# A set's four groups of states side by side in one row, products with C by halves of the time axis, in an SSM and FP4 FFN kernel

## The chip, the cores and the metric

One core of a Trainium2 chip runs the whole program. The metric is the device time in microseconds (us) of one execution. The kernel before takes 343.71 us (median of three runs, 343.64 to 343.86).

## The reference, cut to what matters

```python
# x: (4, 1024, 128); 16 states per channel
u = silu(conv3(x));  Bc, Cc = split(u @ W_bc + b_bc);  dt = softplus((u @ W_dt + b_dt) @ W_dtp + b_dtp)
h[t] = exp(A * dt[t]) * h[t-1] + Bc[t] * x[t] * dt[t]      # for each of 128 channels and 16 states
y[t] = sum_n Cc[t, n] * h[t, n] + x[t] * Dcoeff
x1 = layernorm(x + y)
out = layernorm(x1 + fp4_linear(silu(fp4_linear(x1, w_gate)) * fp4_linear(x1, w_up), w_down))
# fp4_linear: blocks of 16 of both operands are rounded to the FP4 grid, then multiplied
```

## The kernel before, in words

The 4096 rows are eight units of 512 time steps (UNIT), two to a batch. The 128 channels times 16 states are 16 groups (GROUPS) of 128 rows: four sets (SETS) of four groups (QUADS); one group holds 32 channels times four states. Each engine has its own instruction list, written out by hand as `step(b, a, s, f, g, h, p)` with 16 slots `k`; the dictionary `AT` (line 84) says in which slot an operation stands on its engine. In step i the scans of unit s = i run; a and b are the units after it, being prepared; f, g and h are the units one, two and three before it, whose norm, quantised FFN and output run in the gaps. An engine works through its list in order and waits at semaphores, so a slot is an order, not a time.

The parts that matter here:

- **ScalarE (ACT)**, line 541: `decay` writes exp(A dt) of one group to one of three PSUM banks.
- **VectorE (DVE)**, line 1122: `times_b` makes B x dt of one set (`db`) from the bank `ps_b` and the replicated dt x. `scan` (line 1133) runs the recurrence of one group over 512 steps, its second operand from PSUM, and writes `states`. Set m of `times_b` stands in slots 15 (of the step before), 3, 7 and 11. Line 1089 is the limiting of FP4 codes (`h quant 5` of unit g in slot 8).
- **GpSimd (POOL)**, line 869: `times_c` multiplies two groups of states with C (`c_rep`), 1024 elements a partition, in each odd slot, after two more scans. Beside it POOL does the elementwise steps of both quantisations: lines 904, 893, 898, 912 for x of unit f, lines 918, 893, 898, 928 for the hidden layer of unit g (its sum in slot 13, its codes, line 898, in slot 15 behind the last product, `hq` in slot 0 of the next step).
- **TensorE (PE)**, line 1401: `sum_states` adds a set's products over its states into `ps_y` with four matmuls. The sums of the last two sets stand in slot 0 of the next step; there they are followed by `spread_b` (line 1452) of set 1, which fills `ps_b` for the next `times_b`.

`states0` holds 16 groups, `states1` six in a ring; `product` holds two sets. In the last step the last set is multiplied with C on DVE (`times_last_c`, line 1210), and PE goes on with `sum_of_last`.

Of the kernel before, what the change touches and what calls it, by code (L numbers as in the profile page):

```python
# [51 lines left out]
def bank_of(unit, k):  # L52
# [9 lines left out]
PRODUCTS = 2 * SET_PAIRS  # L62
ODD_STATES = 6
X1 = 3
# [18 lines left out]
AT = {  # L83
    "pe x": 11, "pe conv": (13,), "pe z": 15, "pe B": (13, 1, 5, 10), "pe C": (5, 6, 8, 10),
    "pe sum": (8, 11, GROUPS, GROUPS), "pe r": 2, "pe xq": 12, "pe gate": (13, 13, 14, 14),
    "pe up": (15, 15, GROUPS, GROUPS), "pe hq": 4, "pe down": (7, 8), "act x": 12, "act window": 15,
    "act C": (4, 7, 9, 10), "act r": 0, "act r variance": 3, "act x1": 3, "act xq": 12, "act hq": 3,
    "act variance": 10, "act y": 11, "act x square": 7, "act h square": 7, "dve db": (15, 3, 7, 11), "dve dtx": 1,
    "dve tiles": (GROUPS, GROUPS, GROUPS + 1, GROUPS + 1),
    "dve x quant": {0: (4, False), 1: (5, True), 2: (5, False), 5: (9, False)},  # L90
    "dve h quant": {0: (1, False), 1: (4, False), 2: (5, True), 5: (8, False)}, "pool x norm": 3, "pool xq": 8,
    "pool h norm": 4, "pool h sum": 13, "pool h codes": 15, "pool hq": GROUPS,
}


FIRST = {**AT,
    "pe x": 0, "pe conv": (1, 2), "pe z": 3, "pe C": (7, 9, 10, 11), "act x": 0, "act window": 4,
    "act C": (7, 8, 9, 11), "dve dtx": 6,
}
# [78 lines left out]


def over(t, n):  # L180

    return t.rearrange("p (a t) -> p a t", a=1).broadcast_to([t.shape[0], n, t.shape[1]])


def build(nc, x, conv_w, w_bc, b_bc, w_dt, b_dt, w_dtp, b_dtp, a_log, dcoeff, w_gate, w_up, w_down, out):
# [6 lines left out]
    with ctx:  # L192
# [50 lines left out]
        db = [sb(f"db{j}", [128, QUADS, UNIT]) for j in range(DB)]  # L243
        states = [sb("states0", [128, GROUPS, UNIT]), sb("states1", [128, ODD_STATES, UNIT])]
        product = sb("product", [128, PRODUCTS, 2, UNIT])

        conv_0 = product[:, 0, 0, :]
        wdt_t, wdtp = (states[1][0:RANK, 3, i * D:(i + 1) * D] for i in range(2))

# [34 lines left out]
        def flat(t):  # L284
            return t.rearrange("p q d -> p (q d)")
# [4 lines left out]

        spare = flat(states[0][:])
        in_use = 3 * TILES * INNER + TILES * 3 * 128
# [33 lines left out]

        last_states = [states[1][:], dt_rep[0][:].rearrange("p c i t -> p (c i) t"), c_rep[0][:]]

        def groups(s, k, n):

            if s.first < UNITS - 1:
                t = states[s.first % 2]
                k %= t.shape[1]
                return t[:, k:k + n, :]
            for t in last_states:
                if k < t.shape[1]:
                    return t[:, k:k + n, :]
                k -= t.shape[1]

# [516 lines left out]
        def _(pool):  # L856
# [143 lines left out]
        def _(dve):  # L1000
# [132 lines left out]
            def scan(s, k, p):  # L1133
                ring = states[p].shape[1]

                if s.first == UNITS - 1 and k >= ring:

                    if k == ring + 2 * QUADS:
                        dve.wait_ge(product_done, s.at(PAIRS))
                elif p == 1 and k >= ring:  # L1140
                    dve.wait_ge(product_done, s.at(PAIRS, (k - ring) // 2 + 1))
                elif s.beyond(2):
                    dve.wait_ge(product_done, s.at(PAIRS, (k - ring - GROUPS) // 2 + 1))
# [5 lines left out]
                nc.vector.tensor_tensor_scan(  # L1149
                    out=groups(s, k, 1)[:, 0, :], data0=ps_decay[BANK_OF[s.at(GROUPS, k)]][:],  # L1150
                    data1=db[k // QUADS % DB][:, k % QUADS, :],
                    initial=states[0][:, k, UNIT - 1:UNIT] if p else 0.0,
                    op0=ALU.mult, op1=ALU.add).then_inc(scan_done, 1)
# [56 lines left out]
            def times_last_c(s, k):  # L1210


                j = k // 2
                dve.wait_ge(scan_done, s.at(GROUPS, k + 1))
                dve.wait_ge(prep_evac, s.at(PREP_EVAC, PREP_EVAC))
                dve.wait_ge(sum_done, s.at(SETS, (j - PRODUCTS) // SET_PAIRS + 1))
                nc.vector.scalar_tensor_tensor(
                    out=product[:, j % PRODUCTS, k % 2, :], in0=ps_prep[:], scalar=bbc_rep[:, 1, SETS - 1:SETS],
                    in1=groups(s, k, 1)[:, 0, :],
                    op0=ALU.add, op1=ALU.mult).then_inc(last_product, 1)  # L1220
# [136 lines left out]
        def _(pe):  # L1357
# [43 lines left out]
            def sum_states(s, m, p):  # L1401
# [186 lines left out]
            def tail(f, g, h, p):  # L1588
                def sum_of_last():

                    m = SETS - 1
                    for c in range(QUADS):
                        pe.wait_ge(last_product, c + 1)
                        last = nc.tensor.matmul(ps_y[c * E:(c + 1) * E, :], gather[:],
                                                product[:, (m * SET_PAIRS + c // 2) % PRODUCTS, c % 2, :],
                                                start=False, stop=True)
# [101 lines left out]
```

## Time and profile before

| | |
|---|---|
| runs, median | 343.71 us |
| the profiled execution | 346.96 us, of which its span on the core 345.2 us |
| DVE busy | 302.5 us (88%) |
| POOL busy | 268.8 us (78%) |
| PE busy, weight loads | 263.9 us (76%), 131.0 us (38%) |
| ACT busy | 248.0 us (72%) |
| products with C on POOL (line 878) | 139.6 + 7.3 us in 62 instructions |
| scans on DVE (line 1149) | 151.4 us of DVE, more with the last unit's |
| chain that ended last | POOL 45%, DVE 16%, issue 12%, PE 12%, ACT 9% |

Busy time is that of instructions on an engine. The middle 60% of the span consists of steps that repeat each 35 us; the rest is a head of about 20 us in which nothing is there yet to scan, and a tail of some 45 us after the last scan. A step begins for DVE with the first scan of its unit. The chain of waits is followed back from the last instruction; where two engines are both busy without a gap, it stays on the one that it is on, so its shares don't tell by themselves which of the two bounds.

### The profile page before, as it was taken

To read this page: it belongs to the slowest core of one execution; us is meant where nothing else is said; L and a number is where in the kernel's file an instruction comes from. 1 tells how busy PE (TensorE), PEld (TensorE's weight loads), DVE (VectorE), ACT (ScalarE), POOL (GpSimd) and SP (SyncE) were. 2 spreads that over 40 slices of the span, in tenths; PEclk is the share of its full clock that TensorE was granted. 3 is DMA by queue.
4 is the path that set the end of the run, shared out by engine and by line. 5 is a ranking of instruction groups with operands and counts; after the bars stand their busy time and mean duration, and the time that the engine had idled before them with its cause. 6 is when DMAs were issued, how large, how long until landed. Compare 5 with 4: busy or idle time off the path is not lost.

```text
span 345.2 us, 3946 instructions
## 1 busy us (share of the span) xinstructions
PE 263.9 (76%) x1130; PEld 131.0 (38%) x1130; DVE 302.5 (88%) x327; ACT 248.0 (72%) x538; POOL 268.8 (78%) x146
## 2 busy tenths in 40 slices
PE   2679976678758879798999888787849667967683
PEld 1223322224313434353534344334324433355582
DVE  3868998999999999999999999999996999756920
ACT  3466889658855987989879988888874866354434
POOL 0084665688279998999899999999999799846632
PEclk9956999989996999989899999999987995969678
DMA  3680663800380028021802190109010001000002
GB/s 50 151 205 0 139 139 76 197 0 0 71 184 22 3 54 191 0 61 34 195 17 62 38 206 1 30 19 207 19 31 2 0 0 31 2 0 12 19 2 62
DMA packets 19262, 21.86 MB, mean 63 GB/s; under 512 B 6112, under 2 KB 15144, under 8 KB 19240
## 3 DMA queue, kind: packets, MB, share of 16 engines
q1 hardware_dynamic: 18520, 21.05, 26.9%
q10 hardware_dynamic: 720, 0.56, 0.9%
q8 instruction: 9, 0.15, 0.2%
q14 instruction: 13, 0.11, 0.1%
HBM read 2.72 MB, written 2.10 MB: 14 GB/s over the span
## 4 chain that ended last, share of the span: by engine, by line
POOL 45%; DVE 16%; issue 12%; PE 12%; ACT 9%; DMA 1%; ACTq 1%; SPq 1%; DVEq 0%; POOLq 0%
POOL product L878 22%; DVE states L1149 6%; DVE db L1129 6%; POOL qh_norm L918 4%; POOL qh_magic L898 4%; POOL qh_norm L893 4%; POOL hq L928 4%; ACT ps_decay L548 2%; ACT L538 2%; POOL qx_norm L904 2%; POOL qx_magic L898 2%; POOL qx_norm L893 2%; POOL xq L912 2%; PE ps_prep L1437 1%; DMA dt_rep<-dtx 1%
## 5 line engine op out<-in xcount | busy, mean ns | idle before, releaser
L878 POOL TENSOR_TENSOR product<-states,c_rep 128x1024 f32<-128x1024 f32 x59 | 139.6, 2383 | 24.8 <-DVE states L1149 21.9
L548 ACT ACTIVATE ps_decay<-dt_rep,aneg 128x512 f32<-128x512 f32 x128 | 87.1, 691 | 25.6 <-DVE states L1149 18.4
L1149 DVE TENSOR_TENSOR_SCAN states<-ps_decay,db 128x512 f32<-128x512 f32 x64 | 74.9, 1201 | 0.3
L1129 DVE SCALAR_TENSOR_TENSOR db<-ps_b,bbc_rep,dt_rep 128x2048 f32<-128x2048 f32 x31 | 72.1, 2326 | 1.4 <-PE ps_b L1456 1.4
L1149 DVE TENSOR_TENSOR_SCAN states<-ps_decay,states,db 128x512 f32<-128x512 f32 x54 | 66.6, 1260 | 1.0 <-ACT ps_decay L548 1.0
L1450 PE MATMUL ps_prep<-u_feat,wbc_rep 128*128 128x512 f32 x56 | 33.4, 680 | 11.8 <-ACT c_rep L625 11.2
L1456 PE MATMUL ps_b<-u_feat,wbc_rep 128*128 128x512 f32 x64 | 38.1, 680 | 5.1 <-DVE db L1129 5.1
L1414 PE MATMUL ps_y<-product,gather 128*32 128x512 f32 x248 | 33.5, 629 | 4.0 <-POOL product L878 4.0
L538 ACT ACT_TABLE_LOAD x25 | 32.1, 1283 | 0.5
L1495 PE MATMUL ps_f<-gate_t,xq_t 128*128 128x352 f32 x48 | 19.7, 537 | 6.8 <-ACT hidden L632 5.7
L625 ACT ACTIVATE c_rep<-ps_prep,bbc_rep 128x512 f32<-128x512 f32 x28 | 19.2, 684 | 7.3 <-PE ps_prep L1450 7.3
L1437 PE MATMUL ps_prep<-x_feat,tap_diag 128*128 128x512 f32 x42 | 21.8, 653 | 2.3 <-issue 1.3
L1541 PE MATMUL ps_f<-ident,hq 128*128 128x128 f32 (+1 forms) x60 | 10.1, 292 | 12.3 <-POOL hq L928 9.4
L1187 DVE TENSOR_TENSOR hidden<-hidden,ps_f 128x352 f32<-128x352 f32 x26 | 13.1, 515 | 7.3 <-PE ps_f L1501 5.2
L928 POOL TENSOR_TENSOR hq<-qh_magic,qh_scale 128x1408 f32<-128x1408 bf16 x7 | 18.1, 2583 | 0.6
L1450 PEld LDWEIGHTS ps_prep<-u_feat,wbc_rep 128*128 128x128 f32 x56 | 9.3, 202 | 24.2 <-ACT c_rep L625 21.9
L1456 PEld LDWEIGHTS ps_b<-u_feat,wbc_rep 128*128 128x128 f32 x64 | 11.3, 206 | 18.5 <-issue 10.5
L1501 PE MATMUL ps_f<-up_t,xq_t 128*128 128x352 f32 x48 | 18.3, 512 | 0.0
L918 POOL TENSOR_TENSOR qh_norm<-hidden,qh_inv 128x1408 f32<-128x1408 f32 x7 | 18.1, 2592 | 0.0
L898 POOL TENSOR_TENSOR qh_magic<-qh_norm,qh_magic 128x1408 bf16<-128x1408 f32 x6 | 17.2, 2870 | 0.1
L893 POOL TENSOR_TENSOR qh_norm<-qh_norm,qh_magic 128x1408 f32<-128x1408 f32 x6 | 17.2, 2859 | 0.0
L1527 PE MATMUL ps_f<-down_t,hq_t 128*128 128x128 f32 (+1 forms) x120 | 16.7, 275 | 0.0
(237 smaller groups left out, 506.1 us busy)
## 6 DMA issues: line engine op xcount, KB each, us to landing
dt_rep<-dtx SPq DMA_DIRECT2D x124, 128.0 KB, 2.4
x_tok<-in_L_attn_x SPq DMA_DIRECT2D x8, 256.0 KB, 2.9
out<-y_out SPq DMA_DIRECT2D x7, 256.0 KB, 2.3
dt_rep<-dtx ACTq DMA_DIRECT2D x4, 128.0 KB, 3.7
out<-y_out SPq DMA_DIRECT2D x2, 128.0 KB, 2.0
hidden<-in_L_ffn_w_down SPq DMA_DIRECT2D x1, 176.0 KB, 3.5
x_feat<-in_L_attn_x SPq DMA_DIRECT2D x8, 0.5 KB, 2.1
hidden<-in_L_ffn_w_gate SPq DMA_DIRECT2D x1, 128.0 KB, 2.8
```

The lines of the kernel that those rows point to most:

```text
L538: act.add_instruction(mybir.InstLoadActFuncSet(act_func_set_id=which, name=nc.get_next_instruction_name(), engine=mybir.EngineType.Activat ...
L548: nc.scalar.activation(ps_decay[BANK_OF[i]][:], dt_rep[p][:, c, 0, :], ACT.Exp, scale=aneg[:, c, m:m + 1]).then_inc(decay_done, 1)
L878: nc.gpsimd.tensor_tensor(product[:, j % PRODUCTS], groups(s, 2 * j, 2), over(c_rep[p][:, j // SET_PAIRS, :], 2), ALU.mult).then_inc(produ ...
L893: order.mark(nc.gpsimd.tensor_tensor(b.norm[:, 0:width], b.norm[:, 0:width], b.magic[:, 0:width], ALU.add))
L898: order.mark(nc.gpsimd.tensor_tensor(b.magic[:, 0:width], b.norm[:, 0:width], b.magic[:, 0:width], ALU.subtract))
L918: nc.gpsimd.tensor_tensor(blocked(qh.norm[:]), blocked(flat(hidden[:])), spread_out(qh.inv[:]), ALU.mult).then_inc(h_norm_done, 1)
L928: nc.gpsimd.tensor_tensor(blocked(flat(hq[:])), blocked(qh.magic[:]), spread_out(qh.scale[:]), ALU.mult).then_inc(hq_done, 1)
L1129: nc.vector.scalar_tensor_tensor(out=db[m % DB][:], in0=over(ps_b[:], QUADS), scalar=bbc_rep[:, 0, m:m + 1], in1=dt_rep[p][:, :, 1, :], op ...
L1149: nc.vector.tensor_tensor_scan(out=groups(s, k, 1)[:, 0, :], data0=ps_decay[BANK_OF[s.at(GROUPS, k)]][:], data1=db[k // QUADS % DB][:, k % ...
L1414: last = nc.tensor.matmul(ps_y[c * E:(c + 1) * E, :], gather[:], product[:, (m * SET_PAIRS + c // 2) % PRODUCTS, c % 2, :], start=False, s ...
L1450: nc.tensor.matmul(ps_prep[:], wbc_rep[:, 1, m], u_feat[o][:], start=True, stop=True).then_inc(prep_mm, 1)
L1456: nc.tensor.matmul(ps_b[:], wbc_rep[:, 0, m], u_feat[o][:], start=True, stop=True).then_inc(b_mm, 1)
```

## The change

The states of a set are laid out time step by time step, the four groups' values of one time step next to each other (16 bytes). A scan writes its 512 values with a stride of four elements; the product of a set is contiguous again, and is made in two instructions of 256 time steps times four groups, in which the value of C is repeated four times (`beside`) where it was a row repeated twice (`over`). Both need all four scans of the set, and both stand in slots 3, 7, 11 and 15, one before and one after the other operations of that slot. PE's sums read `product` with a stride of four elements, `times_last_c` reads and writes so. `states1` holds eight groups, and its ring is given free set by set. Slots: PE's `spread_b` of set 1 from 1 to 2, r from 2 to 4, x's transposes from 12 to 13, the fourth gate matmul from 14 to 15; ACT's r from 0 to 1; DVE's `h quant 5` from 8 to 11; POOL's h sum from 13 to 12; and three slots of the first unit.

```diff
-ODD_STATES = 6
+SIDE = QUADS
+ODD_STATES = 8
...
-    "pe x": 11, "pe conv": (13,), "pe z": 15, "pe B": (13, 1, 5, 10), "pe C": (5, 6, 8, 10),
-    "pe sum": (8, 11, GROUPS, GROUPS), "pe r": 2, "pe xq": 12, "pe gate": (13, 13, 14, 14),
+    "pe x": 11, "pe conv": (13,), "pe z": 15, "pe B": (13, 2, 5, 10), "pe C": (5, 6, 8, 10),
+    "pe sum": (8, 11, GROUPS, GROUPS), "pe r": 4, "pe xq": 13, "pe gate": (13, 13, 14, 15),
-    "act C": (4, 7, 9, 10), "act r": 0, "act r variance": 3, "act x1": 3, "act xq": 12, "act hq": 3,
+    "act C": (4, 7, 9, 10), "act r": 1, "act r variance": 3, "act x1": 3, "act xq": 12, "act hq": 3,
-    "dve h quant": {0: (1, False), 1: (4, False), 2: (5, True), 5: (8, False)}, "pool x norm": 3, "pool xq": 8,
-    "pool h norm": 4, "pool h sum": 13, "pool h codes": 15, "pool hq": GROUPS,
+    "dve h quant": {0: (1, False), 1: (4, False), 2: (5, True), 5: (11, False)}, "pool x norm": 3, "pool xq": 8,
+    "pool h norm": 4, "pool h sum": 12, "pool h codes": 15, "pool hq": GROUPS,
...
+def beside(t, n):
+
+    return t.rearrange("p (t a) -> p t a", a=1).broadcast_to([t.shape[0], t.shape[1], n])
...
-        states = [sb("states0", [128, GROUPS, UNIT]), sb("states1", [128, ODD_STATES, UNIT])]
-        product = sb("product", [128, PRODUCTS, 2, UNIT])
+        states = [sb("states0", [128, GROUPS // SIDE, UNIT, SIDE]), sb("states1", [128, ODD_STATES // SIDE, UNIT, SIDE])]
+        product = sb("product", [128, PRODUCTS * 2 * UNIT])
+        products = product[:].rearrange("p (m t c) -> p m t c", t=UNIT, c=SIDE)
...
             def times_c(s, j, p):
-                pool.wait_ge(scan_done, s.at(GROUPS, 2 * j + 2))
+                m, half = j // SET_PAIRS, slice(j % SET_PAIRS * UNIT // 2, (j % SET_PAIRS + 1) * UNIT // 2)
+                pool.wait_ge(scan_done, s.at(GROUPS, QUADS * m + QUADS))
...
-                nc.gpsimd.tensor_tensor(product[:, j % PRODUCTS], groups(s, 2 * j, 2),
-                                        over(c_rep[p][:, j // SET_PAIRS, :], 2), ALU.mult).then_inc(product_done, 1)
+                nc.gpsimd.tensor_tensor(products[:, m % 2, half], beside_each_other(s, QUADS * m)[:, half],
+                                        beside(c_rep[p][:, m, half], SIDE), ALU.mult).then_inc(product_done, 1)
...
                 for k in range(GROUPS):
-                    if s is not None and k % 2 and (a is not None or k < GROUPS - QUADS):
-                        times_c(s, k // 2, p)
+                    products = s is not None and k % QUADS == QUADS - 1 and (a is not None or k < GROUPS - QUADS)
+                    if products:
+                        times_c(s, k // 2 - 1, p)
                     if g is not None:
                         quant(g, k)
...
                     if h is not None:
                         quant(h, k + GROUPS)
+                    if products:
+                        times_c(s, k // 2, p)
...
                 elif p == 1 and k >= ring:
-                    dve.wait_ge(product_done, s.at(PAIRS, (k - ring) // 2 + 1))
+                    dve.wait_ge(product_done, s.at(PAIRS, ((k - ring) // QUADS + 1) * SET_PAIRS))
...
                 nc.vector.tensor_tensor_scan(
-                    out=groups(s, k, 1)[:, 0, :], data0=ps_decay[BANK_OF[s.at(GROUPS, k)]][:],
+                    out=state(s, k), data0=ps_decay[BANK_OF[s.at(GROUPS, k)]][:],
                     data1=db[k // QUADS % DB][:, k % QUADS, :],
...
                     last = nc.tensor.matmul(ps_y[c * E:(c + 1) * E, :], gather[:],
-                                            product[:, (m * SET_PAIRS + c // 2) % PRODUCTS, c % 2, :],
+                                            product_of(m, c),
                                             start=False, stop=(m == SETS - 1))
```

## Rows read from the trace of the kernel before

**Rows 1.** Windows, step 5: length, busy of PE, PEld, DVE, ACT, POOL

```profile
204.68:239.51 34.83, 29.19 (x141) 14.30 (x141) 34.28 (x34) 30.11 (x67) 34.00 (x17) 1.00 0.30 67
```

**Rows 2.** DVE's timeline: start us, us, engine, line, operation, idle before and releaser

```profile
222.82 1.27 DVE L1149 TENSOR_TENSOR_SCAN states<-ps_decay,states,db 128x512 f32<-128x512 f32 x1
224.01 1.19 DVE L1149 TENSOR_TENSOR_SCAN states<-ps_decay,db 128x512 f32<-128x512 f32 x1
225.65 1.11 DVE L1187 TENSOR_TENSOR hidden<-hidden,ps_f 128x352 f32<-128x352 f32 x2 [0.45 <-PE ps_f L1501]
...
232.10 2.32 DVE L1129 SCALAR_TENSOR_TENSOR db<-ps_b,bbc_rep,dt_rep 128x2048 f32<-128x2048 f32 x1
```

**Rows 3.** POOL's timeline of the same stretch

```profile
223.61 2.85 POOL L893 TENSOR_TENSOR qh_norm<-qh_norm,qh_magic 128x1408 f32<-128x1408 f32 x1
226.43 2.37 POOL L878 TENSOR_TENSOR product<-states,c_rep 128x1024 f32<-128x1024 f32 x1
228.75 2.87 POOL L898 TENSOR_TENSOR qh_magic<-qh_norm,qh_magic 128x1408 bf16<-128x1408 f32 x1
...
239.51 1.06 POOL L904 TENSOR_TENSOR qx_norm<-x,qx_inv 128x512 f32<-128x512 f32 x1 [0.59 <-DVE qx_inv L1077]
```

**Rows 4.** PE there: weights of the last sum, then the matmul for `times_b`

```profile
228.84 0.27 PEld L1414 LDWEIGHTS ps_y<-product,gather 128*32 128x32 f32 x8 [0.58 <-POOL product L878]
229.96 1.12 PE L1456 MATMUL ps_b<-u_feat,wbc_rep 128*128 128x512 f32 x2
```

**Rows 5.** Groups of POOL's instructions: xcount | busy us, mean ns | idle before

```profile
L878 POOL TENSOR_TENSOR product<-states,c_rep 128x1024 f32<-128x1024 f32 x59 | 139.6, 2383 | 24.8 <-DVE states L1149 21.9 <-PE ps_y L1414 2.9
L918 POOL TENSOR_TENSOR qh_norm<-hidden,qh_inv 128x1408 f32<-128x1408 f32 x7 | 18.1, 2592 | 0.0
L893 POOL TENSOR_TENSOR qh_norm<-qh_norm,qh_magic 128x1408 f32<-128x1408 f32 x6 | 17.2, 2859 | 0.0
...
L904 POOL TENSOR_TENSOR qx_norm<-x,qx_inv 128x512 f32<-128x512 f32 x7 | 7.4, 1060 | 7.5 <-DVE qx_inv L1077 7.5
```

**Rows 6.** DVE's timeline at another boundary of steps, and at the last one

```profile
152.85 1.27 DVE L1149 TENSOR_TENSOR_SCAN states<-ps_decay,states,db 128x512 f32<-128x512 f32 x1
...
162.39 2.33 DVE L1129 SCALAR_TENSOR_TENSOR db<-ps_b,bbc_rep,dt_rep 128x2048 f32<-128x2048 f32 x1
...
257.29 1.21 DVE L1149 TENSOR_TENSOR_SCAN states<-ps_decay,db 128x512 f32<-128x512 f32 x1
...
268.22 2.32 DVE L1129 SCALAR_TENSOR_TENSOR db<-ps_b,bbc_rep,dt_rep 128x2048 f32<-128x2048 f32 x1
```

**Rows 7.** Timeline of step 2 about slots 8 to 11

```profile
104.73 0.89 DVE L1089 TENSOR_SCALAR qh_magic<-qh_magic 128x1408 bf16<-128x1408 bf16 x1
...
105.54 1.21 DVE L1149 TENSOR_TENSOR_SCAN states<-ps_decay,db 128x512 f32<-128x512 f32 x1
...
106.83 1.91 PE L1456 MATMUL ps_b<-u_feat,wbc_rep 128*128 128x512 f32 x2
...
108.79 2.35 DVE L1129 SCALAR_TENSOR_TENSOR db<-ps_b,bbc_rep,dt_rep 128x2048 f32<-128x2048 f32 x1 [0.59 <-PE ps_b L1456]
```

**Rows 8.** The same two operations in step 6

```profile
246.12 1.02 PE L1456 MATMUL ps_b<-u_feat,wbc_rep 128*128 128x512 f32 x2
...
248.33 2.32 DVE L1129 SCALAR_TENSOR_TENSOR db<-ps_b,bbc_rep,dt_rep 128x2048 f32<-128x2048 f32 x1
```

**Rows 9.** Timeline of the tail: POOL's hq and PE around it

```profile
298.27 2.58 POOL L928 TENSOR_TENSOR hq<-qh_magic,qh_scale 128x1408 f32<-128x1408 bf16 x1
...
299.84 0.76 PE L1520 MATMUL ps_f<-up_t,xq_t 128*128 128x352 f32 x2
...
300.90 0.66 PE L1541 MATMUL ps_prep<-ident,hq 128*128 128x128 f32 x4 [0.30 <-POOL hq L928]
```

**Rows 10.** Groups of DVE's instructions: a scan, a product of the last set

```profile
L1149 DVE TENSOR_TENSOR_SCAN states<-ps_decay,db 128x512 f32<-128x512 f32 x64 | 74.9, 1201 | 0.3
...
L1217 DVE SCALAR_TENSOR_TENSOR product<-ps_prep,bbc_rep,dt_rep 128x512 f32<-128x512 f32 x2 | 1.5, 750 | 0.1
```

More of the change, by code:

```diff
@@ L90 @@
     "dve x quant": {0: (4, False), 1: (5, True), 2: (5, False), 5: (9, False)},
-    "dve h quant": {0: (1, False), 1: (4, False), 2: (5, True), 5: (8, False)}, "pool x norm": 3, "pool xq": 8,
-    "pool h norm": 4, "pool h sum": 13, "pool h codes": 15, "pool hq": GROUPS,
+    "dve h quant": {0: (1, False), 1: (4, False), 2: (5, True), 5: (11, False)}, "pool x norm": 3, "pool xq": 8,
+    "pool h norm": 4, "pool h sum": 12, "pool h codes": 15, "pool hq": GROUPS,
 }
 FIRST = {**AT,
-    "pe x": 0, "pe conv": (1, 2), "pe z": 3, "pe C": (7, 9, 10, 11), "act x": 0, "act window": 4,
-    "act C": (7, 8, 9, 11), "dve dtx": 6,
+    "pe x": 0, "pe conv": (1, 3), "pe z": 3, "pe C": (6, 9, 10, 11), "act x": 0, "act window": 4,
+    "act C": (7, 8, 10, 11), "dve dtx": 6,
 }
@@ L243, in build @@
         db = [sb(f"db{j}", [128, QUADS, UNIT]) for j in range(DB)]
-        states = [sb("states0", [128, GROUPS, UNIT]), sb("states1", [128, ODD_STATES, UNIT])]
-        product = sb("product", [128, PRODUCTS, 2, UNIT])
-        conv_0 = product[:, 0, 0, :]
-        wdt_t, wdtp = (states[1][0:RANK, 3, i * D:(i + 1) * D] for i in range(2))
+        states = [sb("states0", [128, GROUPS // SIDE, UNIT, SIDE]), sb("states1", [128, ODD_STATES // SIDE, UNIT, SIDE])]
+        product = sb("product", [128, PRODUCTS * 2 * UNIT])
+        products = product[:].rearrange("p (m t c) -> p m t c", t=UNIT, c=SIDE)
+        conv_0 = product[:, 0:UNIT]
+        wdt_t, wdtp = (states[1][0:RANK, 0, :, :].rearrange("p t c -> p (t c)")[:, i * D:(i + 1) * D] for i in range(2))
         r_feat = sb("r_feat", [128, UNIT])
@@ L288, in build @@
         wraw, wquant = flat(hidden[:])[:, 0:WCOLS], flat(hq[:])[:, 0:WCOLS]
-        spare = flat(states[0][:])
+        spare = states[0][:].rearrange("p q t c -> p (q t c)")
         in_use = 3 * TILES * INNER + TILES * 3 * 128
@@ L324, in build, with beside_each_other, state, product_of @@
         last_q = [tail_quant(i, last_gate[i][:, 0:INNER] if i in in_bank else tail_norm[:, i]) for i in range(TILES)]
-        last_states = [states[1][:], dt_rep[0][:].rearrange("p c i t -> p (c i) t"), c_rep[0][:]]
-        def groups(s, k, n):
+        last_states = [states[1][:], dt_rep[0][:].rearrange("p c i t -> p (c i t)")
+                       .rearrange("p (q t c) -> p q t c", t=UNIT, c=SIDE)]
+        def beside_each_other(s, k):
             if s.first < UNITS - 1:
                 t = states[s.first % 2]
-                k %= t.shape[1]
-                return t[:, k:k + n, :]
+                return t[:, k // SIDE % t.shape[1]]
             for t in last_states:
-                if k < t.shape[1]:
-                    return t[:, k:k + n, :]
-                k -= t.shape[1]
+                if k < t.shape[1] * SIDE:
+                    return t[:, k // SIDE]
+                k -= t.shape[1] * SIDE
+        def state(s, k):
+            return beside_each_other(s, k)[:, :, k % SIDE]
+        def product_of(m, c):
+            k = m * QUADS + c
+            return products[:, k // SIDE % (PRODUCTS * 2 // SIDE), :, k % SIDE]
         def gate_bank(f, i):
@@ L1133, in scan @@
             def scan(s, k, p):
-                ring = states[p].shape[1]
+                ring = states[p].shape[1] * SIDE
                 if s.first == UNITS - 1 and k >= ring:
-                    if k == ring + 2 * QUADS:
-                        dve.wait_ge(product_done, s.at(PAIRS))
+                    pass
                 elif p == 1 and k >= ring:
-                    dve.wait_ge(product_done, s.at(PAIRS, (k - ring) // 2 + 1))
+                    dve.wait_ge(product_done, s.at(PAIRS, ((k - ring) // QUADS + 1) * SET_PAIRS))
                 elif s.beyond(2):
-                    dve.wait_ge(product_done, s.at(PAIRS, (k - ring - GROUPS) // 2 + 1))
+                    dve.wait_ge(product_done, s.at(PAIRS, ((k - ring - GROUPS) // QUADS + 1) * SET_PAIRS))
                 dve.wait_ge(decay_done, s.at(GROUPS, k + 1))
@@ L1149, in scan @@
                 nc.vector.tensor_tensor_scan(
-                    out=groups(s, k, 1)[:, 0, :], data0=ps_decay[BANK_OF[s.at(GROUPS, k)]][:],
+                    out=state(s, k), data0=ps_decay[BANK_OF[s.at(GROUPS, k)]][:],
                     data1=db[k // QUADS % DB][:, k % QUADS, :],
-                    initial=states[0][:, k, UNIT - 1:UNIT] if p else 0.0,
+                    initial=states[0][:, k // SIDE, UNIT - 1:UNIT, k % SIDE] if p else 0.0,
                     op0=ALU.mult, op1=ALU.add).then_inc(scan_done, 1)
@@ L1217, in times_last_c @@
                 nc.vector.scalar_tensor_tensor(
-                    out=product[:, j % PRODUCTS, k % 2, :], in0=ps_prep[:], scalar=bbc_rep[:, 1, SETS - 1:SETS],
-                    in1=groups(s, k, 1)[:, 0, :],
+                    out=product_of(SETS - 1, k % QUADS), in0=ps_prep[:], scalar=bbc_rep[:, 1, SETS - 1:SETS],
+                    in1=state(s, k),
                     op0=ALU.add, op1=ALU.mult).then_inc(last_product, 1)
@@ L1594, in sum_of_last @@
                         last = nc.tensor.matmul(ps_y[c * E:(c + 1) * E, :], gather[:],
-                                                product[:, (m * SET_PAIRS + c // 2) % PRODUCTS, c % 2, :],
+                                                product_of(m, c),
                                                 start=False, stop=True)
```

## The prediction

> **What bounds the kernel now.** I read the page first (busy shares, chain), then windows of one step, then the timeline of DVE, POOL and PE at the boundary of two steps, last the tail. The page's chain runs 45% through POOL and invites the thought that POOL is the bound. The window says otherwise: in a step of 34.83 us DVE is busy 34.28 us and POOL 34.00 us [rows 1]. Two engines are full, and the timelines tell which waits for which. DVE's only wait is 0.45 us for a matmul of PE [rows 2]. POOL waits 0.59 us, for DVE's reciprocal [rows 3]. DVE never waits for POOL. So DVE sets the step, and POOL keeps up with about 0.6 us to spare. A cheaper product on POOL buys nothing in the middle, and what must be asked is what the later place of the products makes late.
>
> **The product itself.** Today 1024 elements take 2383 ns [rows 5]. The reads stay contiguous for the states, and C is repeated innermost. The nearest row with an innermost repeat is line 904/918: 1060 ns for 512 and 2592 ns for 1408, so 1.71 ns per further element, and 1060 + 512 x 1.71 = 1.94 us for 1024. That repeat is 16 long, here it is 4, so 1.94 is the low end unless a repeat of 4 is cheaper than one of 16, which nothing suggests. The high end is no gain, 2.36 us, today's in the timeline [rows 3]; a start for each short run of four could even pass that, and each 0.1 us more costs what 0.1 us less saves below. Line 893 (one operand half as wide) takes 2859 ns for 1408, between the two. I take 1.94, as the nearest in form. From start to start today's product takes 2.32 us (226.43 to 228.75 [rows 3]), the new one then 1.90.
>
> The Trainium skill, GPSIMD Engine Reference, section 2.1, says that a two-input operation has its operands share one read port and so costs about 2.5 cycles an element, whatever is repeated. An estimate from that page at its 1.2 GHz is 2.1 ns an element, which today's product fits and line 918 does not; by it the product stays as it is.
>
> **The boundary of two steps, where the change costs.** Today the last product needs the last two scans and stands alone ahead of POOL's codes (line 898); its sum follows on PE, and behind that sum in PE's list stands `spread_b` of set 1, which DVE's second `times_b` waits for. In the trace: product until 228.80, PE takes the sum at 228.84, the matmul for `times_b` runs from 229.96 to 231.08, and DVE comes to it at 232.10 [rows 2 to 4]: 1.0 us to spare. After the change both halves need scan 15, and the codes stand between them. The new path, from the end of scan 15 (222.82 + 1.27 = 224.09 [rows 2]): start of POOL 0.08 (an estimate from the gap between engines), product 1.90, codes 2.82 (the 2.85 to 2.87 us operations take 2.82 from start to start [rows 3]), product 1.94, start of PE 0.04, sum 1.12, matmul 1.12 [rows 4], start of DVE 0.05: 9.07 us. DVE's own path to that `times_b` is 232.10 - 224.09 = 8.01 us [rows 2]. So DVE waits 1.06 us. At another boundary its path is 162.39 - 152.85 - 1.27 = 8.27 us [rows 6], wait 0.80. Moving `spread_b` from slot 1 to 2 alters nothing, the sum is ahead of it either way.
>
> How often: the codes exist from step 2 on, and the last boundary has a path of 268.22 - 257.29 - 1.21 = 9.72 us [rows 6], longer than 9.07, because its hidden tiles come late. That leaves the ends of steps 2, 3, 4 and 5: four boundaries, at a mean of the two waits of 0.93: **+3.7 us**. Boundaries 0 and 1 have no codes: 2.82 less, no wait. The work that starts from DVE or from the sum (r, x1, the quantisations) moves with the wait; PE's r one matmul later (1.12) meets a DVE that is 1 us later too.
>
> **Step 2, slots 8 to 11.** `h quant 5` moves from ahead of `times_b` of set 3 to behind scan 11. In step 2 that `times_b` waits 0.59 us for PE already, whose matmul ends at 106.83 + 1.91 = 108.74 [rows 7]. This is set by ACT and PE (slow there), not by DVE. The 0.81 us of the moved operation (104.73 to 105.54 [rows 7]) was cover for that wait; it now stands behind it: **+0.8 us**. In step 6 the matmul ends at 247.14 and DVE comes at 248.33 [rows 8], 1.19 us of slack, which pays for it; there, and in the steps like it, zero, at most 0.3.
>
> **The tail.** In the last step POOL's two products before h's sum are 2 x 0.42 us shorter, so `hq` ends some 0.9 us before today's 300.85. But PE's list has the up matmul ahead of its transposes, until 300.60 [rows 9]; the transposes start 0.3 us earlier and no more: **-0.3 us**. `times_last_c` now reads and writes with a stride. It takes 0.75 us, and if it fell to a scan's pace 1.20 us [rows 10], four would cost 1.8 us, all on the path to the last sum. Zero and 1.8 are the ends; I take zero, as its other operand comes from PSUM and one stream from SBUF is left.
>
> **Scans and sums with a stride.** A scan takes 1.20 us for 512, 2.35 ns an element [rows 10], where `times_b` writes one element every 2.32/2048 = 1.14 ns [rows 2]. A write that costs twice would still hide in the scan's pace. I take zero. The sums read with a stride; no row shows such a matmul. From nothing to a doubling (+1.12 each); zero taken, the doubling is a rival.
>
> The ring of `states1` grows from six to eight groups and is freed set by set: scan 8 waits for set 0, whose second half ends before set 1's scans do; scan 12 for set 1. No wait. The rest of the slots (gate, xq, first unit) pass nothing that the rows show to be late: zero.
>
> **The sum.** 3.7 + 0.8 - 0.3 = +4.2 us. The profiled execution has 345.2 us of span in 346.96; with +4.2 it would be 349.4 in 351.2. The median of the runs is 343.71, 3.25 under that, so **347.9 us**.
>
> **The rivals.**
> 1. *The product is no quicker* (2.36 us). For it: a repeat of four is short. Two products in each of four paths, 8 x 0.42 = +3.4 us: 351.3 us. Between the two, with line 893's rate, about 349.4. POOL would then have no idle time.
> 2. *PE's strided reads cost.* Every value that a sum reads lies 16 bytes behind the one before; if that halves the rate, a sum takes 2.24 instead of 1.12 us, 4 x 1.12 = 4.5 at the boundaries and 1.1 in the tail: 347.9 + 5.6 = 353.5 us. Against it: the four matmuls read the same 16 bytes side by side. The Trainium skill (SBUF — State Buffer, the note on SBUF cachelines) has this rule: lines are 16 bytes, and a read that meets a new line each time pays a penalty; by it the sums, the scans and `times_last_c` would all be slower.
> 3. *Scans slow down*, if a strided write costs three times 1.14 ns: 3.42 x 512 = 1.75 us, +0.55 each on the engine that bounds, for 128 scans +70 us: 414 us. Against it: a factor of two still hides.
> 4. *Not slower: the boundary closes.* Without products, the path is 9.07 - 3.84 = 5.23 us, so it fits into 8.14 (the mean of the two) if two products take 2.9 us, 1.45 us each: the point from which it decides. It would need 1.3 ns an element, under every row. Then 343.7 + 0.8 - 0.3 = 344.2 us; and if step 2's PE also comes sooner and `hq`'s whole 0.9 us counts, 342.8. The page's chain, so much on POOL, speaks for it, the waits [rows 2, 3] against.
>
> **How the numbers follow.** The forecast (346.9 to 349.5) has 0.46, rival 1 0.16, rival 2 0.12, rival 3 0.05, rival 4 0.21: 0.09 at 344.2, 0.12 at 342.8. 0.2% (0.7 us) is about what a measurement of this kernel can tell from no change; so faster 0.12, same 0.09, slower 0.79. The range leaves out rival 3 and the lower half of rival 4, and runs from 343.6 to 353.8.
>
> **What would show it.** In the profile after: product (line 878's successor) near 1.94 us; POOL busy some 30.6 us of each step, 34.0 less 8 x 0.42; DVE's `times_b` of set 1 with about 1 us idle ahead of it, released by PE `ps_b`, four times; between the two last products 2.9 us of codes; scans at 1.20 and 1.27, sums at 1.1. Wrong would be: `times_b` without a wait there (then the path is shorter than I think), or longer scans, or sums with long matmuls, or a step still of 34.8 us.

## The result and the profile after

The changed kernel takes 357.81 us, the kernel before 343.78 us in the same comparison: a ratio of 1.039, 95% interval 1.035 to 1.043. Slower, as forecast, but by 14.0 us and not by 4.2, and above the range (343.6 to 353.8). One of the four executions of after took 1318.5 us, for a reason that nothing here shows; the ratio is taken over the other three. The profiled execution of after took 356.63 us with a span of 354.8.

The page of after, busy times:

```profile
PE 278.4 (78%) x1130; PEld 124.2 (35%) x1130; DVE 304.7 (86%) x327; ACT 247.9 (70%) x538; POOL 248.0 (70%) x146
```

POOL does 20.8 us less than before (268.8), PE 14.5 us more (263.9), DVE 2.2 us more (302.5). DVE, which sets the step, now idles 50.1 us of its span where it idled 42.7: it waits more. The groups of POOL, PE and DVE of after, each with its count, its busy time and mean, and the idle time ahead:

```profile
L895 POOL TENSOR_TENSOR product<-states,c_rep 128x1024 f32<-128x1024 f32 x60 | 121.3, 2039 | 62.9 <-DVE states L1168 62.7
...
L1433 PE MATMUL ps_y<-product,gather 128*32 128x512 f32 x248 | 61.3, 1071 | 7.6 <-POOL product L895 7.5
...
L1149 DVE SCALAR_TENSOR_TENSOR db<-ps_b,bbc_rep,dt_rep 128x2048 f32<-128x2048 f32 x31 | 72.3, 2331 | 11.1 <-PE ps_b L1475 11.0
L1168 DVE TENSOR_TENSOR_SCAN states<-ps_decay,db 128x512 f32<-128x512 f32 x64 | 75.0, 1204 | 0.3
L1236 DVE SCALAR_TENSOR_TENSOR product<-ps_prep,bbc_rep,dt_rep 128x512 f32<-128x512 f32 x4 | 4.6, 1154 | 0.1
```

Line 895 is before's product with C (2383 ns [rows 5]): 2039 ns, the gain is there. Line 1168 is the scan: 1204 ns against 1201 [rows 10], so the scan's write with a stride costs nothing here. Line 1236 is `times_last_c`: 1154 ns against 750 [rows 10]. And line 1433, the sums on TensorE, takes 1071 ns a record in the mean, where before had 629:

```profile
L1414 PE MATMUL ps_y<-product,gather 128*32 128x512 f32 x248 | 33.5, 629 | 4.0 <-POOL product L878 4.0
```

Both means hold stretches of different clock; the medians, which the view of one line gives, are 1077 and 592 ns. The wait of 11.0 us is DVE's `times_b` for `ps_b`.

A boundary of two steps, DVE's timeline of after (start, length, ..., idle before and its releaser):

```profile
229.70 1.27 DVE L1168 TENSOR_TENSOR_SCAN states<-ps_decay,states,db 128x512 f32<-128x512 f32 x1
...
237.86 1.21 DVE L1168 TENSOR_TENSOR_SCAN states<-ps_decay,db 128x512 f32<-128x512 f32 x1
241.01 2.35 DVE L1149 SCALAR_TENSOR_TENSOR db<-ps_b,bbc_rep,dt_rep 128x2048 f32<-128x2048 f32 x1 [1.94 <-PE ps_b L1475]
```

POOL and PE there:

```profile
231.05 2.01 POOL L895 TENSOR_TENSOR product<-states,c_rep 128x1024 f32<-128x1024 f32 x1 [0.40 <-DVE states L1168]
233.02 2.88 POOL L915 TENSOR_TENSOR qh_magic<-qh_norm,qh_magic 128x1408 bf16<-128x1408 f32 x1
235.84 2.04 POOL L895 TENSOR_TENSOR product<-states,c_rep 128x1024 f32<-128x1024 f32 x1
...
234.99 1.98 PE L1433 MATMUL ps_y<-product,gather 128*32 128x512 f32 x8
237.93 1.99 PE L1433 MATMUL ps_y<-product,gather 128*32 128x512 f32 x8 [0.96 <-POOL product L895]
239.85 1.13 PE L1475 MATMUL ps_b<-u_feat,wbc_rep 128*128 128x512 f32 x2
```

This is the predicted path, link by link: scan 15 ends at 230.97, product, codes, product, sum, matmul, and DVE goes on at 241.01. It is 10.04 us long, not 9.07: the sum takes 1.92 us to the start of the next matmul and not 1.12 (+0.80), the products together 0.18 more. DVE's wait for `ps_b` appears seven times (1.75, 0.79, 1.81, 1.94, 1.81, 1.94 and 1.01 us), not four, also at the first two boundaries, where no codes stand in the path.

### The profile page after: what moved, and what is told of

It is laid out like the page before. It is cut to its first block, busy times and chain, and to the rows that moved or that the text cites. A ratio compares the mean times of both kernels' runs of the same rounds, so it can differ in the third digit from the quotient of the medians.

```text
span 354.8 us, 3946 instructions
## 1 busy us (share of the span) xinstructions
PE 278.4 (78%) x1130; PEld 124.2 (35%) x1130; DVE 304.7 (86%) x327; ACT 247.9 (70%) x538; POOL 248.0 (70%) x146
## 4 chain that ended last, share of the span: by engine, by line
PE 24%; POOL 24%; DVE 19%; issue 12%; ACT 11%; SPq 6%; DMA 2%; DVEq 0%; ACTq 0%; POOLq 0%
POOL product L895 13%; DVE states L1168 7%; PE ps_y L1433 6%; DVE db L1149 6%; SPq L508 5%; POOL qh_magic L915 3%; PE ps_b L1475 3%; POOL qh_norm L910 2%; DVE dt_rep L1168 2%; ACT hq_t L724 2%; ACT r_feat L671 2%; ACT ps_decay L564 2%; DMA dt_rep<-dtx 1%; PE ps_f L1520 1%; POOL qx_magic L915 1%
## 5 line engine op out<-in xcount | busy, mean ns | idle before, releaser
L895 POOL TENSOR_TENSOR product<-states,c_rep 128x1024 f32<-128x1024 f32 x60 | 121.3, 2039 | 62.9 <-DVE states L1168 62.7
L1168 DVE TENSOR_TENSOR_SCAN states<-ps_decay,db 128x512 f32<-128x512 f32 x64 | 75.0, 1204 | 0.3
L1168 DVE TENSOR_TENSOR_SCAN states<-ps_decay,states,db 128x512 f32<-128x512 f32 x56 | 69.1, 1261 | 1.2 <-ACT ps_decay L564 1.2
L1433 PE MATMUL ps_y<-product,gather 128*32 128x512 f32 x248 | 61.3, 1071 | 7.6 <-POOL product L895 7.5
L1475 PE MATMUL ps_b<-u_feat,wbc_rep 128*128 128x512 f32 x64 | 35.3, 634 | 8.7 <-DVE db L1149 8.7
L1469 PE MATMUL ps_prep<-u_feat,wbc_rep 128*128 128x512 f32 x56 | 30.4, 624 | 6.8 <-ACT c_rep L641 5.7
L1514 PE MATMUL ps_f<-gate_t,xq_t 128*128 128x352 f32 x48 | 18.7, 514 | 11.7 <-ACT hidden L648 7.5
L1456 PE MATMUL ps_prep<-x_feat,tap_diag 128*128 128x512 f32 x42 | 19.5, 595 | 1.3 <-issue 1.3
L1433 PEld LDWEIGHTS ps_y<-product,gather 128*32 128x32 f32 x248 | 5.9, 109 | 35.2 <-POOL product L895 25.3
L689 ACT ACTIVATE r_feat<-ps_y 128x512 f32<-128x512 f32 x8 | 4.8, 597 | 19.0 <-PE ps_y L1433 14.8
L1520 PE MATMUL ps_f<-up_t,xq_t 128*128 128x352 f32 x48 | 17.2, 482 | 0.1
```

Source lines behind the costliest of these rows:

```text
L895: nc.gpsimd.tensor_tensor(products[:, m % 2, half], beside_each_other(s, QUADS * m)[:, half], beside(c_rep[p][:, m, half], SIDE), ALU.mult ...
L1168: nc.vector.tensor_tensor_scan(out=state(s, k), data0=ps_decay[BANK_OF[s.at(GROUPS, k)]][:], data1=db[k // QUADS % DB][:, k % QUADS, :], i ...
L1456: last = nc.tensor.matmul(ps_prep[:], tap_diag[:, tap], x_feat[o][:, tap:tap + UNIT], start=(tap == 0), stop=(tap == 2))
L1469: nc.tensor.matmul(ps_prep[:], wbc_rep[:, 1, m], u_feat[o][:], start=True, stop=True).then_inc(prep_mm, 1)
L1475: nc.tensor.matmul(ps_b[:], wbc_rep[:, 0, m], u_feat[o][:], start=True, stop=True).then_inc(b_mm, 1)
L1520: nc.tensor.matmul((ps_f1, ps_f2)[i % 2][:, 0:INNER], xq_t[:, i * 128:(i + 1) * 128], up_t[:], start=True, stop=True).then_inc(up_mm, 1)
```

## The experiments

Theory: one path from scan 15 to the next `times_b`, lengthened by the codes (the new order) and by sums that read with a step of four elements (the new layout). Rivals: only one of the two counts; the slots; the strided writes.

**Order undone in the changed kernel.**

```diff
                     if products:
                         times_c(s, k // 2 - 1, p)
+                        times_c(s, k // 2, p)
...
-                    if products:
-                        times_c(s, k // 2, p)
```

> The changed kernel, with POOL's codes of h (slot 15) behind both products of the last set instead of between them. Theory A (one path sets the step's boundary: scan 15, product, codes, product, sum, matmul for times_b, times_b): the path falls by the 2.8 us of the codes, from 10.0 to 7.2 us, below DVE's own 8.0 to 8.3, so the five waits of DVE with codes in front (1.81, 1.94, 1.81, 1.94, 1.01) go and those of the first two boundaries (1.75, 0.79) stay: 357.8 - 8.5 = 349.3 us. Theory B (PE is simply too full, since its sums take twice as long): nothing of that moves, 357 to 358 us.

Measured: 351.98 us, ratio 1.024 (1.014 to 1.033). The waits for `ps_b` fall from 11.0 to 6.5 us: 1.76 at the first boundary and 0.73 to 0.84 at each of the six others. So the order costs 5.8 us by the medians and 5.2 by the ratios; the executions of this run lie between 349.1 and 355.4 us, so either is good to 2 or 3 us. Theory A had the five waits with codes gone. They are not: something is left at every boundary, though no codes stand between the products anywhere.

**Sums with contiguous reads in the changed kernel** (they add other products than the reference does).

```diff
-                                            product_of(m, c),
+                                            product_row(m, c),   # product[:, at:at + UNIT]
```

> The changed kernel, but the sums of a set read its four rows of the product buffer as contiguous quarters instead of with a stride of four (so they add other products than the reference's; all the work is there). The last unit's last sum keeps the stride. Both theories agree that matmuls of 0.59 us come back in place of 1.07. Theory A: the path at a boundary is 0.85 us shorter, seven waits fall by it (the one of 0.79 goes), 5.8 us, so about 352 us; about 1 us of DVE wait a boundary is left, as the prediction had it. Theory B: all waits on ps_b go, 346 us.

Measured: 352.64 us, ratio 1.029 (1.022 to 1.037); a sum record 630 ns. Its sums have the price that the prediction took, and its waits are near the predicted ones (1.06 or 0.80 at four boundaries):

```profile
DVE db L1154 <- PE ps_b L1480: 5.6, 6, 1.4
```

They are 1.37, 1.00, 0.89 and 1.01 at the four boundaries with codes, 0.22 in step 2, and 1.07 at the first boundary, of which more below. Taking the stride out gives back 5.2 us by the medians and 3.4 by the ratios, again good to 2 or 3 us; the waits for `ps_b` alone fall by 5.4 us.

**The stride alone in the kernel before** (its sums add other products too).

```diff
-                                            product[:, (m * SET_PAIRS + c // 2) % PRODUCTS, c % 2, :],
+                    row = product[:, m * SET_PAIRS % PRODUCTS:m * SET_PAIRS % PRODUCTS + SET_PAIRS]\
+                        .rearrange("p j i t -> p (j i t)").rearrange("p (t c) -> p t c", c=QUADS)[:, :, c]
```

> The kernel before, with its order and layout, but the sums read the product buffer with a stride of four elements (other products than the reference's are added; all the work is there). Theory A: the path of the kernel before has 1.0 us to spare and the sum takes 0.85 more, so 0 to 1 us in the boundaries and up to 1 us in the tail: 343.8 to 345.8 us. Theory B: PE has 4 us more in each step, some 1.5 us or more of it shows in each, 354 us or more.

Measured: 349.61 us, ratio 1.020 (1.013 to 1.026). Nothing but the address pattern of one operand has changed, and the mean record goes from 629 to 1072 ns (the median from 592 to 1077):

```profile
L1416 PE MATMUL ps_y<-product,gather 128*32 128x512 f32 x248 | 60.2, 1072 | 1.5 <-POOL product L878 1.5
```

My expectation that 1.0 us to spare would hide it was wrong. A boundary in this run's timelines of PE and DVE, and one of before's PE; `x16` is both sums:

```profile
158.88 3.78 PE L1416 MATMUL ps_y<-product,gather 128*32 128x512 f32 x16
162.60 1.13 PE L1457 MATMUL ps_b<-u_feat,wbc_rep 128*128 128x512 f32 x2
...
163.76 2.35 DVE L1129 SCALAR_TENSOR_TENSOR db<-ps_b,bbc_rep,dt_rep 128x2048 f32<-128x2048 f32 x1 [0.80 <-PE ps_b L1457]
```

```profile
228.10 1.92 PE L1414 MATMUL ps_y<-product,gather 128*32 128x512 f32 x16
229.96 1.12 PE L1456 MATMUL ps_b<-u_feat,wbc_rep 128*128 128x512 f32 x2
```

PE has no gap in either. Two sums, of sets 2 and 3, stand in slot 0 behind the up matmuls, so the second path to `ps_b` is PE's own list, and on it the stride counts twice. The two sums take 229.96 - 228.10 = 1.86 us in before and 162.60 - 158.88 = 3.72 us here: 1.86 us more against 1.0 to spare, 0.8 left over; the waits are 0.74 to 0.80 at five boundaries and 1.12 at the sixth, 5.0 us in all.

**The order alone on the layout of before.** The products stay [pair, 2, time] with `over`, but both of a set wait for its four scans and the codes stand between them; the slots are the new ones.

```diff
-                pool.wait_ge(scan_done, s.at(GROUPS, 2 * j + 2))
+                pool.wait_ge(scan_done, s.at(GROUPS, QUADS * (j // SET_PAIRS) + QUADS))
```

> The kernel before with its layout and its products of two groups over all 512 time steps, but all slots of the changed kernel and its order: both products of a set wait for all four scans, and POOL's codes stand between the last two. Theory A: product 2.32, codes 2.82, product 2.36, sum 1.12, matmul 1.12 and 0.17 of starts are 9.9 us against 8.1 of DVE, 1.8 us at four boundaries and some 0.5 at the others: 343.8 + 8 = 352 us. Theory B (the strided reads are the cause): 344 to 345 us.

Measured: 362.03 us, ratio 1.054 (1.047 to 1.061), worse than the whole change and 10 us over theory A. With products of 2.35 us the path is some 0.7 us longer than the change's, and POOL comes to it late (product at 162.24, scan 15 ended at 161.88). Theory A left out more: the first boundary waits 2.95 us and step 2 1.83 us for `ps_b`, and three times a scan waits 0.9 us for POOL's product, because this kernel kept the ring of six groups. The profiled execution took 3.9 us more than the median, so it counts for the kind of the loss and not for its size. One boundary, PE and DVE:

```profile
165.90 1.07 PE L1417 MATMUL ps_y<-product,gather 128*32 128x512 f32 x8
169.77 1.64 PE L1417 MATMUL ps_y<-product,gather 128*32 128x512 f32 x8 [2.81 <-POOL product L878]
171.34 2.08 PE L1459 MATMUL ps_b<-u_feat,wbc_rep 128*128 128x512 f32 x2
...
173.45 2.35 DVE L1132 SCALAR_TENSOR_TENSOR db<-ps_b,bbc_rep,dt_rep 128x2048 f32<-128x2048 f32 x1 [3.47 <-PE ps_b L1459]
```

PE waits 2.81 us for the product, and the sum and the matmul behind it take 1.64 and 2.08 us instead of 1.07 and 1.13: 1.5 us more. Windows of PE, the clock in the column after the busy time:

```profile
166.00:170.00 4.00, 1.19 (x12) 1.00 0.00 0
170.00:174.00 4.00, 4.00 (x16) 0.57 0.92 199
```

The granted clock is 1.00 in the first window and 0.57, nearly its lower level of 1.2 GHz, in the second, behind the idle stretch. At this boundary the late product is paid twice. In the changed kernel PE's wait for the product is 0.96 us, and its clock is 1.00 from 234 to 242 us, over the boundary shown.

**The last sum behind the spread of B in the changed kernel**, and then the same with the codes last.

```diff
-    "pe sum": (8, 11, GROUPS, GROUPS)
+    "pe sum": (8, 11, GROUPS, GROUPS + 2)
```

> Of the changed kernel, only the place of the last set's sum: two slots later on TensorE, so that the spread of B for the new step's second set stands ahead of it. Theory A (times_b waits because two strided sums of 1.9 us and the last products stand ahead of its matmul on TensorE, one chain from scan 15 on): the wait for ps_b is gone at all seven boundaries (11.0 us to under 2), and the time falls from 357.8 by most of that; the block's result comes some 1.1 us later, which may bring back up to 1 us a boundary as a wait for x1. 345 to 350 us. Rival B (the sums' longer reads cost wherever TensorE does them, not by this wait): at least 355 us.

> Both orders mended in the changed kernel: the codes stand behind the last products, and the last sum stands behind the spread of B. Theory A: no wait for ps_b at any boundary, no later x1 than with the first alone; what is left over the kernel before is times_last_c (4 x 0.40 = 1.6 us) and the first products: 344 to 347 us. Rival B (the slots laid out anew cost for themselves, in steps 2 and 7): 348 to 351 us, with waits other than for ps_b.

Measured: 356.85 us, ratio 1.037 (1.029 to 1.046), and 354.83 us, ratio 1.034 (1.027 to 1.040). Theory A's numbers (345 to 350, and 344 to 347) hold in neither. The first fits rival B's number (at least 355) but not its mechanism, since the wait only changed its place; the second lies above both of its theories. The waits of DVE in the second:

```profile
DVE qx_amax L1074 <- ACT x L703: 8.6, 7, 1.4
DVE hidden L1205 <- PE ps_f L1519: 4.9, 7, 2.1
...
DVE db L1148 <- PE ps_b L1474: 2.7, 6, 0.8
```

At the boundaries the wait for `ps_b` goes, and one for x1 of 0.9 to 1.4 us comes. I had allowed up to 1 us for it, as if x1 had slack. It had none. Take the boundary near 200 us, and count from the start of its `dtx`: DVE comes to x1 after 201.82 - 195.14 = 6.7 us in before, and ACT has ended x1 just then (201.79). In the changed kernel x1 ends after 208.07 - 200.27 = 7.8 us, and this didn't show, since DVE was held up by `ps_b`. With the last sum behind the spread of B it ends after 206.99 - 199.17 = 7.8 us too: the spread only fills the 0.9 us that PE had waited for the last product. With the codes last as well the product is early, PE has no such gap, and the overtaken sum really is later: x1 ends after 204.77 - 198.04 = 6.7 us with the codes last alone, and after 207.65 - 199.84 = 7.8 us with both:

```profile
203.63 1.14 ACT L703 ACTIVATE x<-ps_f,rstd 128x128 f32<-128x128 f32 x4
...
206.52 1.13 ACT L703 ACTIVATE x<-ps_f,rstd 128x128 f32<-128x128 f32 x4
```

So two chains leave the same two sums on PE, one to `times_b` and one over r to x1, and neither has anything to spare. What helps is less work ahead of both.

**Both costs out of the changed kernel**: contiguous sums (again other products) and codes last.

> The changed kernel with both suspected costs taken out: the sums read contiguous rows (they add other products than the reference does), and the codes stand behind both last products. Theory A (the loss is the two together, the order's 2.9 us of codes and two sums of 1.96 us on one chain): the boundaries fall back to those of before, 174.9 us between the first and the last dtx on the boundaries of steps 1 to 6 where before has 175.0 and the change 183.0; the time is 343 to 346.5 us, with times_last_c (1.6 us) left. Rival B (the new slots or the strided writes have a price of their own): over 348 us.

Measured: 347.90 us, ratio 1.011 (1.004 to 1.018), just above theory A's 346.5 and just under rival B's 348, so the time alone decides for neither. From the first to the last `dtx` shown it takes 229.97 - 54.16 = 175.8 us, where before takes 175.0 and the change 183.0. No `times_b` waits at a boundary with codes any more. The last unit's last sum kept its stride in this run, without a loss that shows: from the end of the last product on DVE to the end of the span it takes 47.0 us, and 49.1 in before. What is left are three things. `times_last_c` costs 4 x 0.40 = 1.6 us. The first boundary has a wait of its own:

```profile
58.16 2.35 DVE L1153 SCALAR_TENSOR_TENSOR db<-ps_b,bbc_rep,dt_rep 128x2048 f32<-128x2048 f32 x1 [1.07 <-PE ps_b L1479]
```

and in step 2 `times_b` waits 0.99 us, 0.4 more than in before's layout (0.59).

**The slots alone**: the changed kernel with the tables `AT` and `FIRST` of before.

> The changed kernel with the slot tables of the kernel before; layout, product and order stay. Theory A (the slots carry nothing of the loss; they moved r and the second set's B by a slot or two): 356 to 359 us, as the change. Rival B (the new slots cost, first of all those of r and of h quant 5 in step 2): under 355 us. Rival C (they had been laid out to soften the new order, and the old ones are worse with it): over 360 us.

Measured: 359.69 us, ratio 1.044 (1.038 to 1.050). The interval overlaps the change's own (1.035 to 1.043): the new slots carry nothing of the loss that shows. The waits for `ps_b` are 11.2 us with the old ones, 11.0 with the new.

**How far the step matters.** The kernel before with sums that read every second, and every third, element (other products again).

```diff
+                    row = product[:, (m * SET_PAIRS + c // 2) % PRODUCTS]\
+                        .rearrange("p i t -> p (i t)").rearrange("p (t c) -> p t c", c=2)[:, :, c % 2]
```

> The kernel before; its sums read the product with a step of two elements (8 bytes) instead of one. It adds other products than the reference does. Theory A (TensorE reads lines of 16 bytes, and with a step of four elements each gives one of the four): two elements of each line are used, so the sum takes 1.12 to 1.5 us a set where the step of four took 1.96; the time is 343.6 to 346. Rival B (any step but one halves the rate): 1.9 us and more a set, 349.6 us as with the step of four.

> The kernel before; its sums read with a step of three elements (12 bytes) and add other products than the reference does. A step of 1 and of 2 elements took 592 and 635 ns a record of the sums, of 4 elements 1072. Theory A (the price follows how many of the bytes that a step spans are used, from two elements on): about 850 ns, between the two. Rival B (a threshold at 16 bytes): 590 to 640 ns. Rival C (anything over 8 bytes is slow): 1050 to 1090 ns.

Measured: every second element 342.81 us, ratio 0.996 (0.992 to 1.001), 635 ns a record; every third 854 ns a record, 342.49 us in a single run. The group of the sums with every second element:

```profile
L1416 PE MATMUL ps_y<-product,gather 128*32 128x512 f32 x248 | 34.0, 635 | 2.3 <-POOL product L878 2.3
```

and with every third

```profile
L1416 PE MATMUL ps_y<-product,gather 128*32 128x512 f32 x248 | 47.1, 854 | 2.8 <-POOL product L878 2.8
```

These are means over stretches of different clock (and the 592 in the expectation is a median). The medians of a record, with a step of 4, 8, 12 and 16 bytes, are 592, 612, 845 and 1077 ns. So 8 bytes cost 3%, and from there each further 4 bytes some 230 ns. The Trainium skill (SBUF — State Buffer, the note on SBUF cachelines) says that a line of 16 bytes needs two hits for full bandwidth: two, 1.33 and one hit a line order these rows as they came out. The same note gives four fp32 elements as the step that is still free. That these rows contradict: three cost 1.43 times, four 1.82 times.

**Two groups side by side, not four.** The changed layout with `SIDE = 2`, and the order and slots of before: a pair's states lie next to each other, C is repeated twice, one product is again one pair over the whole time axis, and the sums step by 8 bytes.

```diff
-SIDE = QUADS
+SIDE = 2
...
-                nc.gpsimd.tensor_tensor(products[:, m % 2, half], beside_each_other(s, QUADS * m)[:, half],
-                                        beside(c_rep[p][:, m, half], SIDE), ALU.mult).then_inc(product_done, 1)
+                nc.gpsimd.tensor_tensor(products[:, j % PRODUCTS], beside_each_other(s, 2 * j),
+                                        beside(c_rep[p][:, j // SET_PAIRS], SIDE), ALU.mult).then_inc(product_done, 1)
```

> The changed kernel's layout with two groups of states lying element by element in a row, not four, and with the order and slots of the kernel before: one product for each pair of groups over the whole time axis, C repeated twice. Theory A (the product is quicker where neighbouring elements use the same C, and what undid it was the sum with a step of four and the order): the product falls below 2.37 us, to 2.04 if a repeat of two is enough; with the sum at a step of two as the run beside this one shows it, 342 to 344.5 us if that is near 1.12 us a set, 347 to 350 if it is 1.9. Rival B (the product's gain is due to the repeat of four): 2.3 to 2.4 us a product, and 344 to 346 us or, with the slow sum, 350.

Measured: 340.95 us, ratio 0.993 (0.990 to 0.996): faster than both kernels, by 0.7% against before, with an interval that lies wholly under 1. Its groups:

```profile
L894 POOL TENSOR_TENSOR product<-states,c_rep 128x1024 f32<-128x1024 f32 x60 | 129.1, 2165 | 29.5 <-DVE states L1164 26.2 <-PE ps_y L1429 3.1
...
L1429 PE MATMUL ps_y<-product,gather 128*32 128x512 f32 x248 | 33.5, 630 | 1.6 <-POOL product L894 1.6
...
L1232 DVE SCALAR_TENSOR_TENSOR product<-ps_prep,bbc_rep,dt_rep 128x512 f32<-128x512 f32 x4 | 3.0, 751 | 0.1
```

The product keeps nearly two thirds of its gain (2165 of 2383 and 2039 ns), the sum (612 ns in the median) and `times_last_c` are back near or at their price, and no `times_b` waits at a boundary. That little comes of 13.6 us less work on POOL agrees with the reading that DVE sets the step. How much of the 0.7% is the product's own is open: the run with a step of two elements on before's layout stands at 0.996 without it, and the two intervals overlap.

## Why the prediction was wrong

**DVE is the bound, POOL keeps up: right.** POOL lost 20.8 us of work and the kernel got slower; the pairs, with 13.6 us less on POOL, gained 0.7%.

**The product: right in kind.** 1.94 was taken, the timeline has 2.01 and 2.04, the group 2.04. That is 0.07 to 0.10 a product, 0.18 for both on the path, their starts with them. By the Trainium skill (GPSIMD Engine Reference, section 2.1) and the prediction's estimate from it, 2.1 ns an element, the product was to stay as it is, and it did not. That today's product fits this figure was a loose reading: 2383 ns are 2.33 ns an element, and the new 2039 ns are 1.99.

**The boundary path: right in its links, wrong in one term.** With contiguous sums, as the prediction had them, the four boundaries waited 0.89 to 1.37 us, 4.3 us in all, where 3.7 was said (0.80 to 1.06 each), and moving the codes gave back 4.7 us there (352.64 to 347.90). In the changed kernel as it is they are worth 5.8 us. The term that failed is the sum at 1.12 us.

**The sums with a stride: the step that failed.** "From nothing to a doubling; zero taken" was argued from the four matmuls that read the same 16 bytes side by side. That saved nothing: a record takes 1077 ns and not 592 in the median, and a whole sum 1.98 us and not 1.07. The rival had this mechanism, and its 5.6 us is about what the stride is worth in all: 5.2 us given back when it is undone in the changed kernel, 6.0 us added when it is put alone into before (349.61 against 343.57). Of the three operations that it named as slower by the note on cachelines, the sums and `times_last_c` are, and the scans are not (1204 against 1201 ns). That its sum fits is luck in part. It charged one sum of 1.12 us at four boundaries. The runs show 0.8 to 0.93 us for a sum, a second sum in a row in slot 0, and, wherever the last product comes early, a path on PE alone that binds at all boundaries but the first. By the waits, the stride adds 3.2 us at the four boundaries with codes and 2.5 us at the first two and the last, where the rival had nothing. Its time of 353.5 us fell short also for the terms below. [Rows 4] show the weights of the last sum waiting 0.58 us for the product, and 1.0 us to spare behind it. The row of PE's two sums back to back, shown above, was not read; it would have given 2 x 0.93 against 1.0 at once, also where no codes stand.

**"Boundaries 0 and 1 have no codes, no wait": wrong.** They waited 1.75 and 0.79 us. Boundary 1 is the pair of sums again: 0.80 with the codes last, none with contiguous sums. Boundary 0 has a second cause, since 1.07 us stay with contiguous sums. After the first unit no hidden tiles stand on DVE between scan 15 and `times_b`. Scan 15 ends at 51.98 there (the product starts at 52.06), and `times_b` could have begun at 57.44, 5.5 us later. Two products of 2.0, a sum and a matmul take 6.2 us even with a contiguous sum. The DVE path of 8 us was carried over from later boundaries to one where it is shorter.

**The last boundary.** "9.72 us, no wait" held with contiguous sums; with strided ones it waits 1.01 us.

**Step 2.** +0.8 us was said for the moved `h quant 5`, on top of a wait that before has there. In the profile of after `times_b` starts at 109.22 without any wait. What differs is PE's clock: the matmul ahead takes 1.02 us in after, where the clock from 105 to 109 us is 1.00 and PE was busy 2.86 us of the 4 us before; in before it takes 1.91 us at a clock of 0.50, its lower level of 1.2 GHz, behind 4 us in which PE was busy 0.03 us. In the two runs with contiguous sums it takes 1.58 and 1.91 us, and `times_b` waits 0.22 and 0.99 us. So the term stood on a slow stretch that the changed kernel does not have; the move itself was never tested alone.

**The tail.** Of the -0.3 us nothing can be seen beside the rest. `times_last_c` was taken at zero, with 1.8 us as the upper end: it came to 1.6 us. The reason given, that only one stream came from SBUF, left out that this stream steps by 16 bytes, and the product that it writes too. Which of the two costs is open.

**The sum put right.** Against the profiled execution of before, 3.2 us over its median, the difference of the spans is 9.6 us. A better yardstick is the run with a step of two elements, before's kernel in all that costs time, span 341.6: 13.2 us less than the change's 354.8. Of these, waits for `ps_b` are 11.0 - 0.6 = 10.4 us and `times_last_c` is 1.6 us, which leaves some 1.2 without a cause shown. The longer last sum is hardly in it: from the end of the last product on DVE to the end of the span it takes 47.7 us, and 47.5 in the yardstick. The 14.0 us between the medians is that, within 1 us. In the prediction's terms: the four boundaries with codes 7.5 us and not 3.7, the first two and the last 3.6 and not 0, step 2 nothing and not 0.8, `times_last_c` 1.6 and not 0.

## What to carry to other kernels

Whoever transposes a layout to make one operation cheap has to price every other reader of it, on the engine that has the least to spare at that moment, and count how many of these readers stand in a row. Halfway can be enough: two elements side by side kept nearly two thirds of the product's gain and cost the reader 3%. When a wait is removed by letting one consumer overtake another, look first how much the overtaken one has to spare; if that is nothing, the wait only moves.

## What the runs showed of the hardware

- TensorE's moving operand in fp32, 512 columns, median of a record: 592 ns contiguous, 612 with a step of 8 bytes, 845 with 12, 1077 with 16.
- The same step of 16 bytes costs DVE's scan nothing on its write (1204 against 1201 ns), and a scalar-tensor-tensor of 512 that reads and writes with it 54% (1154 against 750 ns); at 8 bytes it has 751.
- A two-operand multiply of 1024 on POOL takes 2383 ns with one operand's rows repeated, 2165 with each element repeated twice and 2039 with four times.
- In one boundary of one run, a wait of 2.8 us for a late product was followed by a stretch at a granted clock of 0.57 in which a sum and a matmul took 3.7 us and not 2.2.
